# A recommendation tower on one core: the pair products move from the whole array in blocks of 32 samples to two 64-column tiles in blocks of 64, and their results are folded into four parts instead of seven

## The reference

```python
e = jnp.stack([tbl_0[ids[:, 0]], ..., tbl_25[ids[:, 25]]], axis=1)          # (512, 26, 128)
combined = jnp.concatenate([r_dense_features[:, None, :], e], axis=1)       # (512, 27, 128)
interactions = jnp.einsum('bfd,bgd->bfg', combined, combined)
iu, ju = jnp.triu_indices(27, k=1)
h = jnp.concatenate([r_dense_features, interactions[:, iu, ju], r_dense_features], axis=1)   # 607 wide
h = jnp.maximum(h @ W_top1 + b_top1, 0.0)      # 607 x 512
h = jnp.maximum(h @ W_top2 + b_top2, 0.0)      # 512 x 256
y = h @ W_top3                                 # 256 x 1
```

## Time and profile before

| | |
|---|---|
| median of 3 runs | 136.37 us (136.06 to 137.54) |
| the profiled execution | 135.71 us, of it 133.9 us from the first instruction to the last |
| PE / DVE / ACT / POOL busy | 105.2 / 78.5 / 70.3 / 83.1 us |
| first products of unit 0 start | 54.49 us |
| mean granted clock of TensorE | 0.987 of 2.4 GHz |

### The profile page before, as it was taken

How to read it: one execution, slowest core, us unless ns; L and a number is a source line. 1 busy time by engine, 2 the same in 40 slices (tenths; PEclk the granted TensorE clock), 3 DMA queues, 4 the chain that set the end, 5 groups by cost and what they waited for, 6 DMA issues and landing times.

```text
span 133.9 us, 2251 instructions
## 1 busy us (share of the span) xinstructions
PE 105.2 (79%) x772; PEld 94.9 (71%) x772; DVE 78.5 (59%) x199; ACT 70.3 (52%) x211; POOL 83.1 (62%) x92
## 2 busy tenths in 40 slices
PE   0000559959179799897699999999999997979994
PEld 0000427738067587787599999899998997969992
DVE  6005076867165879199999487479479728095001
ACT  3030165692473984398656098445376751547222
POOL 3278787887778778787787787787777773000000
PEclk9999999999967999999999999999999999999999
DMA  2895654899975442121221221221221221000000
GB/s 46 252 258 183 179 194 151 261 271 258 259 177 162 159 127 64 39 59 39 59 62 40 59 62 45 54 59 48 55 58 43 61 62 40 0 0 5 0 0 0
DMA packets 6041, 13.23 MB, mean 99 GB/s; under 512 B 1823, under 2 KB 2848, under 8 KB 5902
## 3 DMA queue, kind: packets, MB, share of 16 engines
q1 hardware_dynamic: 2668, 7.06, 17.6%
q0 software_dynamic: 2560, 5.25, 15.3%
q10 hardware_dynamic: 802, 0.78, 2.0%
HBM read 13.08 MB, written 0.00 MB: 98 GB/s over the span
## 4 chain that ended last, share of the span: by engine, by line
PE 58%; DMA 18%; SPq 12%; DVE 6%; issue 2%; ACT 2%; DVEq 0%; ACTq 0%
PE gram_ps L484 19%; DMA table_sb<-in_tbl 18%; PE dense_ps L499 14%; SPq L202 9%; PE turn_ps L458 5%; PE dense_ps L508 4%; PE turn_ps L499 4%; PE gram_ps L542 3%; SPq L204 3%; PE gram_ps L544 3%; DVE pairs L425 3%; DVE features_t L166 2%; PE dense_ps L491 2%; PE gram_ps L593 1%; PE dense_ps L516 1%
## 5 line engine op out<-in xcount | busy, mean ns | idle before, releaser
L234 POOL DMA_INDIRECT rows<-in_gathered_tables,row_at x80 | 81.9, 1023 | 28.3 <-issue 24.1
L314 ACT COPY pairs<-gram_ps 27x56 f32<-27x56 f32 (+1 forms) x128 | 31.8, 249 | 15.7 <-PE gram_ps L484 14.3
L425 DVE COPY pairs<-gram_ps 27x56 f32<-27x56 f32 (+1 forms) x128 | 32.6, 254 | 7.9 <-PE gram_ps L484 5.9
L484 PE MATMUL gram_ps<-features_t 128*123 128x108 f32 x256 | 30.3, 272 | 4.1 <-DVE pairs L425 1.9
L484 PEld LDWEIGHTS gram_ps<-features_t 128*123 128x123 f32 x256 | 28.8, 187 | 5.4 <-issue 5.4
L542 PE MATMUL gram_ps<-one_hot,table_hi 125*128 125x512 f32 x48 | 22.5, 468 | 7.8 <-ACT one_hot L267 6.2
L166 DVE COPY features_t<-turn_ps 128x512 f32<-128x512 f32 x16 | 17.1, 1066 | 15.9 <-PE turn_ps L458 15.7
L544 PE MATMUL gram_ps<-one_hot,table_lo 125*128 125x512 f32 x48 | 21.1, 439 | 0.0
L499 PE MATMUL dense_ps<-pairs,w_pairs_sb 128*128 128x128 f32 x168 | 20.8, 275 | 0.0
L499 PEld LDWEIGHTS dense_ps<-pairs,w_pairs_sb 128*128 128x128 f32 x168 | 19.7, 192 | 0.1
L542 PEld LDWEIGHTS gram_ps<-one_hot,table_hi 125*128 125x128 f32 x48 | 10.6, 220 | 12.3 <-ACT one_hot L267 7.9
(11 more groups left out here) (43 smaller groups left out, 66.1 us busy)
## 6 DMA issues: line engine op xcount, KB each, us to landing
table_sb<-in_tbl SPq DMA_DIRECT2D x5, 500.0 KB
w_pairs_sb<-in_w_pairs SPq DMA_DIRECT2D x1, 1792.0 KB, 14.8
hot_ids_sb<-in_hot_ids SPq DMA_DIRECT2D x6, 256.0 KB
rows<-in_gathered_tables,row_at POOLq DMA_INDIRECT x80, 2.7
w_dense_sb<-in_w_dense SPq DMA_DIRECT2D x1, 512.0 KB, 17.1
w_sb<-in_w SPq DMA_DIRECT2D x1, 512.0 KB, 24.6
table_sb<-in_tbl ACTq DMA_DIRECT2D x1, 500.0 KB
dense_rows<-in_dense ACTq DMA_DIRECT2D x1, 256.0 KB, 13.6
```

What stands on the lines that cost most here:

```text
L234: pool.indirect_dma_start(rows[:, u, m, :], None, gathered_tables, bass.IndirectOffsetOnAxis(ap=row_at[:, u, m:m + 1], axis=0)).then_inc(r ...
L314: last = act.copy(*pair_block(u, j, k))
L425: last = nc.vector.tensor_copy(*pair_block(u, j, k))
L484: last = nc.tensor.matmul(gram_ps[0:quad_rows, u % 2, q, 0:4 * FEATURES], flat_features[:, b * SLOTS:b * SLOTS + quad_rows], features_t[:, ...
```

## The change

A block of 64 samples takes the place of the unit in the products and the folding; gathers, transposes and placing stay by units of 32. In detail:

- A product takes two samples: 59 stationary columns and 54 moving ones. Products alternate between output partitions 0 to 58 and 64 to 122, that is between the left and the right 64 columns of the array. A block has 32 of them (64 instruction pairs), a buffer of `gram_ps` holds 16 x 64 columns.
- The 27 columns of a sample's block are folded in half. ACT copies columns 0 to 13 of all four j (`plain_pairs`, 16 copies of 27 x 4 x 16 or 27 x 3 x 16). Since the block is symmetric, half of what lies there is double; into those places DVE writes columns 14 to 26, where a mask (`late_rows`, loaded by a DMA of its own) is set: 16 `copy_predicated` of the same shapes (`late_pairs`). They wait for ACT's copies of the same j. `pairs` and `w_pairs` then have four parts instead of seven, and the DMA of `w_pairs` 1,024 KB instead of 1,792.
- `TURN_AFTER` and `LAYER1_AFTER` are written for blocks; `LATE` is gone. Layer 1's relu comes after the fold of the tile's second block.

```diff
-PAIR_PARTS = 7
+COLUMNS = 14
+PAIR_PARTS = 4
...
-TURN_AFTER = {4: 0, 5: 1, 6: 3, 7: 5, 8: 6, 9: 8, 10: 9, 11: 10, 12: 11, 13: 12, 14: 13, 15: 14}
-LAYER1_AFTER = ((0,), (1, 2), (3,), ())
-LATE = {13: 1, 14: 1}
+TURN_AFTER = {0: (4, 5), 1: (6, 7), 2: (), 3: (8, 9), 4: (10, 11), 5: (12, 13), 6: (14, 15), 7: ()}
+LAYER1_AFTER = ((0, 1), (2, 3))
+BLOCK = 2 * UNIT
...
-        gram_ps = psum("gram_ps", [P, 2, quads, P])
+        gram_ps = psum("gram_ps", [P, 2, quads, 64])
...
-                def first_pairs(u):
-                    act.wait_ge(gram_done, u + 1)
-                    for j in (0, 1):
+                def plain_pairs(n):
+                    act.wait_ge(gram_done, n + 1)
+                    for j in range(4):
                         for k in range(4):
-                            last = act.copy(*pair_block(u, j, k))
-                    last.then_inc(pairs_act, 1)
+                            last = act.copy(*pair_block(n, j, k, 0, len(range(k, COLUMNS, 4))))
+                        last.then_inc(pairs_plain, 1)
...
+                for n in range(blocks):
+                    t, v = n // tile_blocks, n % tile_blocks
+                    if t >= 2 and v == 0:
+                        results(t - 2, layer3_at)
+                    plain_pairs(n)
+                    for u in TURN_AFTER[n]:
+                        place_small(u)
+                    if t >= 1 and v == tile_blocks - 1:
+                        layer1_relu(t - 1, layer1_at)
                         layer2_relu(t - 1, layer2_at)
...
-                def other_pairs(u):
-                    dve.wait_ge(gram_done, u + 1)
-                    for j in (2, 3):
-                        for k in range(4):
-                            last = nc.vector.tensor_copy(*pair_block(u, j, k))
-                    last.then_inc(pairs_dve, 1)
+                def late_pairs(n):
+                    for j in range(4):
+                        dve.wait_ge(pairs_plain, n * 4 + j + 1)
+                        for k in range(4):
+                            count = len(range(k, FEATURES - COLUMNS, 4))
+                            dst, src = pair_block(n, j, k, COLUMNS, count)
+                            late = late_sb[32 * k:32 * k + FEATURES, 0:count].rearrange("p (i o) -> p i o", o=1)
+                            last = nc.vector.copy_predicated(dst, late.broadcast_to([FEATURES, count, quads]), src)
+                    last.then_inc(pairs_whole, 1)
+                for n in range(blocks):
+                    late_pairs(n)
+                    for u in TURN_AFTER[n]:
+                        place_large(u)
+                    if n + tile_blocks < blocks:
+                        place_whole(n + tile_blocks)
...
                     for q in range(quads):
-                        b = u % units * UNIT + q * 4
-                        last = nc.tensor.matmul(gram_ps[0:quad_rows, u % 2, q, 0:4 * FEATURES],
-                                                flat_features[:, b * SLOTS:b * SLOTS + quad_rows],
-                                                features_t[:, b:b + 4, 0:FEATURES], start=True, stop=True)
+                        for h in range(2):
+                            b = n % tile_blocks * BLOCK + q * 4 + 2 * h
+                            last = nc.tensor.matmul(gram_ps[64 * h:64 * h + SLOTS + FEATURES, n % 2, q, 0:2 * FEATURES],
+                                                    flat_features[:, b * SLOTS:b * SLOTS + SLOTS + FEATURES],
+                                                    features_t[:, b:b + 2, 0:FEATURES], start=True, stop=True)
                     last.then_inc(gram_done, 1)
...
+                for n in range(blocks):
+                    t, v = n // tile_blocks, n % tile_blocks
+                    products(n)
                     if t >= 2 and v == 0:
                         layer3(t - 2, layer3_at)
+                        pe.wait_ge(y_out, t - 1)
                     if t >= 1:
                         for m in LAYER1_AFTER[v]:
                             layer1_dense(t - 1, m, layer1_at)
                             layer1_pairs(t - 1, m, layer1_at)
+                    for u in TURN_AFTER[n]:
+                        transpose_unit(u)
+                    if t >= 1 and v == tile_blocks - 1:
                         layer2(t - 1, layer2_at)
```

More of the change, by code:

```diff
@@ L62, in pair_places, with dlrm_program @@
                 c = 4 * i + k
-                yield 32 * k + g, i, (c, g) if c < g < FEATURES else None
-def dlrm_program(nc, ids, gathered_tables, hot_ids, hot_tables, dense, w_dense, w_pairs, w2, columns, y):
+                if g >= FEATURES or c >= COLUMNS:
+                    yield 32 * k + g, i, None, False
+                elif c + 1 <= g <= c + 13:
+                    yield 32 * k + g, i, (c, g), False
+                elif c + 14 < FEATURES and g != c + 14:
+                    yield 32 * k + g, i, (min(g, c + 14), max(g, c + 14)), True
+                else:
+                    yield 32 * k + g, i, None, False
+def dlrm_program(nc, ids, gathered_tables, hot_ids, hot_tables, dense, w_dense, w_pairs, w2, columns,
+                 late_rows, y):
     batch, dim = dense.shape
@@ L71, in dlrm_program @@
     n1, n2 = hidden1 // P, hidden2 // P
-    quads = UNIT // 4
+    quads, blocks = BLOCK // 4, batch // BLOCK
+    tile_blocks = P // BLOCK
     n_hot = len(HOT)
@@ L167, in place, with pair_block @@
                  turned_at(u, n).rearrange("p (s b) -> p s b", b=UNIT)).then_inc(placed[n], 1)
[L169 to L178, removed]
+        def pair_block(n, j, k, first, count):
+            at = FEATURES * (j % 2) + first + k
+            src = gram_ps[32 * j:32 * j + FEATURES, n % 2, :, at:at + 4 * (count - 1) + 1:4].rearrange("p q i -> p i q")
+            b = n % tile_blocks * BLOCK + j
+            return pairs[32 * k:32 * k + FEATURES, n // tile_blocks % 2, 0:count, b:b + 4 * (quads - 1) + 1:4], src
         def hot_bank(n):
-            return gram_ps[:, n % 2, 0:4, :].rearrange("p q c -> p (q c)")
+            return gram_ps[:, n % 2, 0:quads // 2, :].rearrange("p q c -> p (q c)")
         layer1_at = [dense_ps[:, m * P:(m + 1) * P] for m in range(n1)]
@@ L188, in dlrm_program @@
         layer3_at = dense_ps[0:1, n2 * P:(n2 + 1) * P]
-        last_layer1_at = [*(turn_ps[:, g, 0:P] for g in range(3)), gram_ps[:, 0, 0, :]]
-        last_layer2_at = [gram_ps[:, 0, 4, :], gram_ps[:, 1, 0, :]]
-        last_layer3_at = gram_ps[0:1, 1, 4, :]
+        free_bank = [gram_ps[:, n, h * (quads // 2):h * (quads // 2) + 2, :].rearrange("p q c -> p (q c)")
+                     for n in range(2) for h in range(2)]
+        last_layer1_at = [*(turn_ps[:, g, 0:P] for g in range(3)), free_bank[0]]
+        last_layer2_at = [free_bank[1], free_bank[2]]
+        last_layer3_at = free_bank[3][0:1, :]
         y_line = y.rearrange("(o b) c -> o (b c)", o=1)
@@ L208, in _ @@
                 sp.dma_start(w2_sb[:, :, :], w2.rearrange("(c p) n -> p c n", p=P)).then_inc(weights_in, 16)
-                with sp.Fori(0, tiles - 2) as t:
+                for t in range(tiles - 2):
                     sp.wait_ge(y_out, t + 1)
-                    sp.dma_start(y_line[:, bass.ds(t * P, P)], y_row[0:1, bass.ds(t * P, P)]).then_inc(y_stored, 16)
+                    sp.dma_start(y_line[:, t * P:(t + 1) * P], y_row[0:1, t * P:(t + 1) * P]).then_inc(y_stored, 16)
                 sp.wait_ge(y_out, tiles)
@@ L247, in place_small @@
                     if u >= units:
-                        act.wait_ge(gram_done, u - units + 1)
+                        act.wait_ge(gram_done, (u - units) // 2 + 1)
                     act.wait_ge(turned[1], u + 1)
@@ L463, in transpose_unit, with products @@
                         transpose_group(u, n)
-                def products(u):
-                    if u < units:
+                def products(n):
+                    if n < tile_blocks:
                         pe.wait_ge(whole_placed, 1)
```

84 lines of the change are left out of this document (24 added, 60 removed).

## The result

The changed kernel takes **151.28 us** (median of 4 runs, 150.3 to 153.82), the kernel before beside it 136.95 (136.06 to 138.34): the ratio is 1.105, with a 95% interval of 1.092 to 1.118. It is slower, by 14.3 us, where 150 was forecast. The profiled execution has a span of 148.5 us against 133.9.

A forecast was written before the change was run, and what follows sets the result against it. PE was taken as the bound between 66 and 120 us. The walked links gave a span of 145.9, 12.0 more than before; median 136.37 + 12.0 + 1.7 for the clock = 150.1, forecast 150, range 136.5 to 158 (8 in 10).

The forecast's parts named there:

- Start: Before the first block's products at 54.5 us nothing the change touches is on the chain; the walk starts there.
- parts 1 and 4: Layer 1 with four parts for seven saves 10.7 us of PE; the serial order of blocks makes the span 12.0 longer.
- The links that I had walked: Times from one block's products to the next, 5.6 to 12.2 us each, then 20.2 from block 7 to the end.
- Part 2, the pair of 53 ns: Products: 64 narrow load-and-matmul pairs a block at 53 ns, 3.4 us, as much as now; bounds 27 and 107 ns.
- my first rival: In the products both array halves work side by side, 1.7 us a block; 137 to 144 us with clock falls; chance 0.30.
- The clock, one fall: PE idles ahead of blocks 1 and 2 and the last layer 2; one fall to half clock on the path, 1.7 us.
- under the rivals with 0.18: Clock falls in nearly every PE idle, five more, 158.6 us; or narrow pairs cost up to 107 ns, 175; chance 0.18.
- Part 3, the masked copy: Fold: DVE's masked copies 0.27 us each, behind ACT's 16 copies of 4.2 us; a block folded 5.7 us after its products.
- upper bound of 0.36: DVE's masked copy in the fold takes at most 0.36 us, from its 352 ns operation on 128 elements from PSUM.
- Faster: Narrower `gram_ps` stripes make ACT's copies cheap, 0.20 instead of 0.263 us; with halves side by side 134.6 us; chance 0.05.

The follow-up runs named there:

- (7): Kernel before with layer 1 summing only four of its seven parts: 186.4 us beside 202.8, instructions late; from unit 8 to the end 44.0 instead of 51.0.
- (1): Changed kernel with each block's products ordered all left half, then all right: 233.1 us beside 209.3 for the kernel before; from block 3 81.1 us, 9.7 more.
- (3): Changed kernel with PE's waits filled by matmuls nobody reads: from block 3 71.6 us against 71.4 without, from block 5 42.9 instead of 45.5.
- (2): Changed kernel with DVE's masked copies replaced by plain ones, mask left out: from block 3 67.0 us, 4.4 less; from block 5 43.8, 1.7 less.
- experiment 5: Changed kernel with transposes and placing ahead of the fold: first run 61.7 us from block 3, 9.7 less; repeated, whole kernel 141.54 us beside 151.6.

## Why the prediction was right

The number (150 for 151.3) and the direction were right for the reason that was given, but inside the sum three terms were off and cancelled. That it came so close is partly luck: the products of the eight blocks took 21.1 us instead of 27.2, and slower layers 2 and a longer fold on DVE filled the gap.

**Start, and parts 1 and 4, the order.** Right. The links that I had walked, against what came (starts of the products above): 8.5 and 7.15; 8.5 and 8.76; 5.6 and 6.22; 12.2 and 13.89; 12.1 and 12.05; 12.2 and 13.28; 12.1 and 12.05; from block 7, 20.2 and 20.2. The sum was 145.9 and the span is 148.5. What was shown: taking the placing out from behind the fold gives back 10.1 of 15.4 us. The saved 10.7 us of PE are real too (7), but they lie beside waits.

**Part 2, the pair of 53 ns.** Wrong, by a choice: I had read 52 out of two load widths, and for one half at a time it is indeed 54 (1). But the halves do overlap, 30 ns. It was my first rival, with 0.30, and the mechanism was its; its time, 137 to 144, was not. The saving is real, since without the overlap the stretch from block 3 takes 9.7 us more (1); what the rival lacked were the longer fold on DVE, and all six falls.

**The clock, one fall.** Wrong: six falls in the loop. Half clock turns 30 ns back to 54, which is why four of the eight blocks took almost the 3.4 us that I had priced by a wrong route. Two of the three layers 2 in the loop took 3.6 us instead of 2.05. It had stood under the rivals with 0.18, as five more falls and 158.6 us; the falls came, all six, and the time didn't, since other terms were smaller. By filling, 2.6 us come back behind block 5 (3). The Trainium skill, TensorE: Matmul & The Clock Gate, table "Why this matters for your kernels", warns of that pattern of bursts and gaps; the granted 0.50 in the rows above agrees.

**Part 3, the masked copy.** Under-priced: 0.383 us for 0.27, over even my upper bound of 0.36. Plain copies of the same shape take 0.247 (2), so the mask itself costs 0.136, 2.2 us a block. It shows at block 4, whose products start 1.84 us behind layer 2, when DVE's placing ends, and at blocks 5 and 7, whose products wait 4.4, and 2.3 with plain copies. The failed bound came from an operation with one input of 128 elements; this one reads two and a mask, and no run says which of them costs.

**The rivals.** Faster was ruled out by the copies: 269 and 243 ns are no cheaper than 253 and 234.

**What the profile was to show.** PE's share of 65% (63%), a transpose waiting 4 us for ACT (3.7 and 3.3), 12.1 us between blocks 4 and 5 (12.05), a slice near 0.5: as said. Not so the 12 between blocks 3 and 4 (13.9) and the 8.5 between 0 and 1 (7.15). I had named "masked copies above 0.3, or pairs off 53 ns" as what would make it wrong; both came, with opposite signs.

What stays open: of the 5.0 us of span by which the better order is still behind the kernel before, 3.4 lie before block 3, where PE waits for DVE's masked folds, and 1.6 between blocks 3 and 5, where it waits for relus behind 16 copies and then runs at half clock. No run whose instructions came in time took either away.

## What to carry to other kernels

Work saved on the engine that bounds a kernel can be lost entirely once the work is grouped more coarsely, if another engine's next small job, which the first one waits for, ends up queued behind the long one: put placing ahead of folding, and walk from one block's start to the next before counting busy time. Take a change apart before keeping it: here one part by itself (two tiles) makes the kernel 2.5% faster, and the bundle makes it 10% slower. When one cost is taken off a ring of three engines, ask at once which of the other two is next; the masks make a fold 2.1 us longer, which cost 4.4 us from block 3 on in one order and nothing that showed there in the other. And compare a stretch with the same stretch of the kernel before, not with nothing: 65 us left of 71 look like a small gain until 58.6 stands beside them.

## What the runs showed of the hardware

- Alternating 32-bit matmuls between the left and right 64 columns: 30 ns for a load and matmul of 59 and 54 columns (1.94 us for 64), against 54 in the same half (3.47); at a granted 0.50, 54 and 98 (3.45 and 6.26).
- A masked copy from PSUM on DVE: 366 and 434 ns for 48 and 64 elements; a plain one 241 and 266.
- PE can stand still for some 60 us more, with nothing named that it waits for ("issue"); that its instructions arrive late is my reading. In experiment 5's first run, while POOL gathered, there was one product in 2.8 us (rows in order of time), and between 85 and 110 us PE was busy for 2.24 of 25 us at a granted 0.50:

```profile
89.01 0.25 PE L483 MATMUL gram_ps<-features_t 128*59 128x54 f32 x1 [2.55 <-issue]
91.81 0.25 PE L483 MATMUL gram_ps<-features_t 128*59 128x54 f32 x1 [2.55 <-issue]
```

```profile
85.00:110.00 25.00, 2.24 (x9) 0.50 0.20 52
```

  The kernel before had it beside them, so it isn't the change. The three runs without it shared one chip, the nine with it lay on four others; whether that is the reason wasn't found.
